# Four transformer layers: the causal mask of the last layer's second score pass moved from matmuls to a select by POOL

## The chip, the cores and the metric

The kernel runs on one core of one Trainium2 chip. The metric is the device time of the whole program in microseconds (us). An execution's time is a little longer than the span of its profile, which runs from the first to the last instruction that was recorded.

## The reference, cut to what matters

The input x is 4 sequences (B = 4) of 256 tokens with 128 features. It passes through four layers: 0 (a transformer block with full attention, 16 heads of 64), 1 (a graph attention), 2 (a conditioned attention, 16 heads of 8) and 3, the last one, where the change lies:

```python
qkv = (x @ Wqkv).reshape(b, t, 3, H, hd)          # H = 16 heads of hd = 8, t = 256
scores = jnp.einsum('bhqd,bhkd->bhqk', q, k) * scale
scores = jnp.where(causal, scores, -jnp.inf)      # causal: key <= query
attn = jax.nn.softmax(scores, axis=-1)
out = jnp.einsum('bhqk,bhkd->bhqd', attn, v)
```

followed by a projection, a residual and an MLP of 512. All of it is in float32 precision; the scores of layers 2 and 3 are products of bfloat16 parts (three parts of each operand).

## The kernel before, in words

Each attention (one layer, one sequence) has 16 heads and computes its scores twice. The **first pass** has the queries on the partitions: PE makes the scores (`scores`, L1427 to L1445) and DVE takes each query's maximum (L1132, which also gives its negative). After each group of four heads DVE turns the negated maxima into two bfloat16 parts (L1149, L1160, L1162), PE transposes them (`shift_rows`, L1461 to L1468), ACT copies them from PSUM to the tile `mT` (L957), and POOL spreads them over four heads in the rows 96 to 127 of the stacked queries (L771). The **second pass** has the keys on the partitions: one matmul per block of 128 keys gives the scores less the maxima (`scores_t`, L1470 to L1486), ACT takes the exponential into `pt` (L965), and PE multiplies `pt` with the values and a column block of ones (`values`, L1512 to L1535). DVE and ACT divide by the sums (L1168, L979, L981, L1176). Two PSUM banks are used for each pass.

In layer 3 the scores above the diagonal are masked. In the first pass a matmul of the identity with `mask_qk` (0 or -1e30) adds to the diagonal block (L1443). In the second pass the key block k meets the queries from 128 k on: key block 0 meets 256 queries, key block 1 meets 128. Each block is followed by a matmul that adds `mask_kq` to its first 128 columns, which are the diagonal block (L1485):

```python
q0 = k * 128 if layer == 3 else 0
at = k * T
dst = bk[:, at:at + T - q0]
ins = nc.tensor.matmul(dst, lhs, rhs[:, q0:T], start=True, stop=(layer == 2))
if layer == 3:
    ins = nc.tensor.matmul(bk[:, at:at + 128], identb[:], mask_kq[:], start=False, stop=True)
```

`pt` has seven slots of 128 x 512 in the layers 2 and 3, and a slot is written again only when PE has used its head (`pt_used`).

The order of the work is fixed in Python. `schedule()` makes a list of steps; in each step every running phase makes one tick. Heavy phases are the attentions, light ones are norms, projections, MLPs, the `qkv` matmuls and the graph layer. An attention has 26 steps i of two ticks each. Every engine walks the same list and so issues its instructions in this order, in order. Step i of an attention holds: first pass of head i; at i = 4, 8, 12 and 16 the transpose, the copy to `mT` and POOL's spread of the group that has just ended; second pass of head i - 6 on PE and its exponential on ACT; every fourth step the values of the four heads up to i - 8. The next attention begins while the former is at its step 15, half a step apart: in its step 4 it makes its first spread, between the former's head 13 and head 14 of the second pass. On PE the first pass of step i + 1 stands behind the second pass of step i.

POOL's queue in layer 3 is the spread (L771), preceded by a wait for everything in the dictionary `latest`, which holds POOL's own earlier results:

```python
for signal, value in latest.items():
    pool.wait_ge(signal, value)
pool.wait_ge(mT_ready, at + 1)
```

and, from light phases, `xb` (L845, once per norm) and the third part of queries and keys (L856, once per `qkv`, before DMAs by SP). POOL makes the constants at the start, `mask_kq` among them (L874, L878).

Of the kernel before, what the change touches and what calls it, by code (L numbers as in the profile page):

```python
# [17 lines left out]
NT = T // 128  # L18
# [365 lines left out]
def cond_seq_kernel(nc, x_t, adj, w0, wqk0, w1, w2, w3, wp2, wproj3, vecs, rows, out_t):  # L384
    with ExitStack() as ctx:
        def sb(name, shape, dt=F32):
            return ctx.enter_context(nc.sbuf_tensor(name, shape, dt))

        def sem(name):
            return ctx.enter_context(nc.semaphore(name))  # L390
# [15 lines left out]
        zero = sb("zero", [128, 1])  # L406
        sel = sb("sel", [128, GH, 128], BF16)
        mask_qk = sb("mask_qk", [128, 128], BF16)
        mask_kq = sb("mask_kq", [128, 128], BF16)
        mask1 = sb("mask1", [128, H, NG])  # L410
        mask2 = sb("mask2", [128, 32])
        silu = sb("silu", [128, 3, B])
# [212 lines left out]
        st_full = sem("st_full")  # L625
        pt_ready = sem("pt_ready")
        pairsum_ready = sem("pairsum_ready")
        pt_used = sem("pt_used")
        sums_ready = sem("sums_ready")
        lnsum_ready = sem("lnsum_ready")  # L630
# [61 lines left out]
        with nc.Block() as block:  # L692
# [55 lines left out]
            def _(pool):  # L748
# [3 lines left out]
                def attention(layer, b):  # L752
                    for i in range(STEPS):
                        yield
                        if 0 <= i - ST_LAG < H and layer == 0:
                            u = U_BASE[layer, b] + i - ST_LAG
                            pool.wait_ge(pt_ready, u + 1)
                            if u >= SUM_RING:
                                pool.wait_ge(pt_used, u - SUM_RING + 1)
                            nc.gpsimd.tensor_tensor(pairsum[:, u % SUM_RING, :], pt[:, pt_slot(u), 0:T],  # L760
                                                    pt[:, pt_slot(u), T:2 * T], ALU.add
                                                    ).then_inc(pairsum_ready, 1)
                            latest[pairsum_ready] = u + 1
                        g = mT_step(layer, i)
                        if g is not None and layer != 0:

                            at = G_BASE[layer, b] + g
# [3 lines that stand above are left out]
                            nc.gpsimd.tensor_copy(stacks[SHIFT_ROW:128, b % ROOMS, 0, GH * g:GH * (g + 1), :],  # L771
                                                  mT[SHIFT_ROW:128, at % 2, :].unsqueeze(1).broadcast_to(
                                                      [128 - SHIFT_ROW, GH, T])).then_inc(mT_spread, 1)
                            pool.wait_ge(mT_spread, at - FIRST_LATE_G + 1)
                        half = {ST_LAG + H // 2: 0, ST_LAG + H: 1}.get(i)
                        if layer == 0 and b >= B - ROOMS and half is not None:

                            for signal, value in latest.items():
                                pool.wait_ge(signal, value)
                            pool.wait_ge(st_full, U_BASE[layer, b] + (half + 1) * H // 2)  # L780
                            for n in range(2):
                                at = (2 * half + n) * H * T // 4
                                nc.gpsimd.memset(big[64:128, b % ROOMS, at:at + H * T // 4], 0.0
                                                 ).then_inc(stack_zero, 1)

                            zeros[0] += 2
                            pool.wait_ge(stack_zero, zeros[0])
                            if half == 1:

                                by_half = sel[SHIFT_ROW:128].unsqueeze(2).broadcast_to([128 - SHIFT_ROW, GH, NT, 128])  # L790
                                for g in range(GROUPS):
                                    keys = stacks[SHIFT_ROW:128, b % ROOMS, 1, GH * g:GH * (g + 1), :]
                                    nc.gpsimd.tensor_copy(keys.rearrange("p h (n t) -> p h n t", n=NT), by_half
                                                          ).then_inc(stack_sel, 1)
                                latest[stack_sel] = GROUPS * (b - (B - ROOMS) + 1)
                                pool.wait_ge(stack_sel, latest[stack_sel])
                        yield
# [72 lines left out]
                for at in (0, GH, DH0, DH0 + GH, SHIFT_ROW, SHIFT_ROW + GH):  # L870
                    step(nc.gpsimd.affine_select(out=sel[:], in_=sel[:], compare_op=ALU.not_equal, fill=1.0, base=-at,
                                                 pattern=[[-1, GH], [0, 128]], channel_multiplier=1))
                step(nc.gpsimd.memset(mask_qk[:], 0.0))
                step(nc.gpsimd.memset(mask_kq[:], 0.0))  # L874

                step(nc.gpsimd.affine_select(out=mask_qk[:], in_=mask_qk[:], compare_op=ALU.is_ge, fill=MASKED, base=0,
                                             pattern=[[-1, 128]], channel_multiplier=1))
                step(nc.gpsimd.affine_select(out=mask_kq[:], in_=mask_kq[:], compare_op=ALU.is_ge, fill=MASKED, base=0,  # L878
                                             pattern=[[1, 128]], channel_multiplier=-1))

                step(nc.gpsimd.memset(mask1[:], 1.0))
                step(nc.gpsimd.affine_select(out=mask1[:], in_=mask1[:], compare_op=ALU.is_ge, fill=0.0, base=0,
                                             pattern=[[-DH, H], [0, NG]], channel_multiplier=1))
# [481 lines left out]
            def _(pe):  # L1365
# [54 lines left out]
                def attention(layer, b):  # L1420
# [49 lines left out]
                    def scores_t(h):  # L1470

                        u = u_base + h
                        g, j = g_base + h // GH, h % GH
                        bk = psum[:, ST_BANK + u % 2, :]
                        pe.wait_ge(pt_ready, u - 1)
                        if j == 0:
                            pe.wait_ge(mT_spread, g - FIRST_LATE_G + 1)
                        for k in range(NT):
                            lhs, rhs = stacks[:, b % ROOMS, 1, h, k * 128:(k + 1) * 128], stacks[:, b % ROOMS, 0, h]
                            q0 = k * 128 if layer == 3 else 0  # L1480
                            at = k * T
                            dst = bk[:, at:at + T - q0]
                            ins = nc.tensor.matmul(dst, lhs, rhs[:, q0:T], start=True, stop=(layer == 2))  # L1483
                            if layer == 3:
                                ins = nc.tensor.matmul(bk[:, at:at + 128], identb[:], mask_kq[:], start=False, stop=True)  # L1485
                        ins.then_inc(st_full, 1)  # L1486

                    def turned_pair(pair):
# [23 lines left out]
                    def values(heads):  # L1512
# [9 lines left out]
                        bk = psum[:, O_BANK + o % 2, :]  # L1522
                        if heads[0] % hpo == 0 and o >= 2:
                            pe.wait_ge(o_done, o - 1)
                        pe.wait_ge(pt_ready, u_base + heads[-1] + 1)
                        for k in range(NT):
                            for h in heads:
                                at = m * (h % hpo)
                                lhs = v0[:, b % ROOMS, k, h * DH0:(h + 1) * DH0] if layer == 0 else vpad[:, vroom, k, h, :]
                                qk = k * q0  # L1530
                                ins = nc.tensor.matmul(bk[at:at + m, qk:T], lhs,  # L1531
                                                 pt[:, pt_slot(u_base + h), k * T:(k + 1) * T - qk],
                                                 start=(k == 0), stop=(k == NT - 1))
                                if k == NT - 1 and layer != 0:
                                    ins.then_inc(pt_used, 1)  # L1535
# [249 lines left out]
```

## Time and profile before

| | us |
|---|---|
| median of 3 runs | 502.93 (501.56 to 503.46) |
| the profiled execution's own time | 503.15 |
| its span | 501.4 |
| PE busy | 412.6 (82%) |
| DVE busy | 309.7 (62%) |
| ACT busy | 281.8 (56%) |
| POOL busy | 175.4 (35%) |

Busy is the time in which an engine had at least one instruction in work. Matmuls overlap each other in PE's pipeline, so that a matmul's duration is longer than the distance to the next one's start; PE's cost of a matmul is that distance. Layer 3's second pass runs from 388.8 us to 483.6 us of the span.

### The profile page before, as it was taken

To read this page: it belongs to the slowest core of one execution; us is meant where nothing else is said; L and a number is where in the kernel's file an instruction comes from. 1 tells how busy PE (TensorE), PEld (TensorE's weight loads), DVE (VectorE), ACT (ScalarE), POOL (GpSimd) and SP (SyncE) were. 2 spreads that over 40 slices of the span, in tenths; PEclk is the share of its full clock that TensorE was granted. 3 is DMA by queue.
4 is the path that set the end of the run, shared out by engine and by line. 5 is a ranking of instruction groups with operands and counts; after the bars stand their busy time and mean duration, and the time that the engine had idled before them with its cause. 6 is when DMAs were issued, how large, how long until landed. Compare 5 with 4: busy or idle time off the path is not lost. (4 is left out here: it accounts for less than half of the span.)

```text
span 501.4 us, 9353 instructions
## 1 busy us (share of the span) xinstructions
PE 412.6 (82%) x3196; PEld 262.0 (52%) x3196; DVE 309.7 (62%) x846; ACT 281.8 (56%) x597; POOL 175.4 (35%) x226
## 2 busy tenths in 40 slices
PE   2777787988989999879996979778788889798974
PEld 2534454555646556445564546344455666576643
DVE  2464686864555646655376675776888777665721
ACT  2243254446545565445755586365767666668674
POOL 2812121331155331593369330641334322321200
PEclk9999899999999999999998899797999999899998
DMA  8920033000000000120002112001322313210000
GB/s 251 248 20 1 2 37 41 8 1 1 0 1 2 0 1 1 56 61 13 0 23 66 41 57 70 3 1 31 95 68 88 99 29 100 77 64 12 3 12 10
DMA packets 34527, 21.25 MB, mean 42 GB/s; under 512 B 22832, under 2 KB 31408, under 8 KB 34096
## 3 DMA queue, kind: packets, MB, share of 16 engines
q1 hardware_dynamic: 34480, 20.65, 15.8%
q8 instruction: 26, 0.43, 0.4%
q14 instruction: 21, 0.17, 0.1%
HBM read 16.97 MB, written 3.67 MB: 41 GB/s over the span
## 5 line engine op out<-in xcount | busy, mean ns | idle before, releaser
L965 ACT ACTIVATE pt<-psum 128x512 f32<-128x512 f32 (+1 forms) x192 | 106.1, 558 | 94.0 <-PE psum L1507 46.1
L1135 DVE TENSOR_REDUCE negm<-psum 128x2 f32<-128x512 f32 x128 | 84.5, 683 | 38.3 <-PE psum L1437 23.4
L760 POOL TENSOR_TENSOR pairsum<-pt 128x256 f32<-128x256 f32 x64 | 46.7, 730 | 141.1 <-ACT pt L965 137.7
L771 POOL COPY big<-mT 32x1024 bf16<-32x1024 bf16 x32 | 33.1, 1035 | 118.7 <-ACT mT L957 118.3
L1483 PE MATMUL psum<-big 128*128 128x256 bf16 (+1 forms) x256 | 50.3, 266 | 4.6 <-POOL big L771 3.4
L1132 DVE TENSOR_REDUCE negm<-psum 128x3 f32<-128x384 f32 x64 | 34.8, 554 | 16.8 <-PE psum L1443 16.1
L1502 PE MATMUL psum<-big 64*128 64x256 f32 x256 | 39.1, 396 | 2.4 <-ACT pt L965 2.2
L1176 DVE TENSOR_TENSOR oT<-psum,rden 128x256 f32<-128x256 f32 x64 | 26.5, 414 | 17.5 <-ACT rden L981 16.9
L1406 PE MATMUL psum<-hT,pt 128*128 128x256 f32 x128 | 34.8, 409 | 2.1 <-DVE negm L1135 1.2
L1531 PE MATMUL psum<-pt,room 128*64 128x256 f32 x256 | 36.5, 408 | 0.0
L1111 DVE COPY big<-psum 128x512 f32<-128x512 f32 x32 | 22.0, 689 | 20.3 <-PE psum L1406 20.1
L1531 PE MATMUL psum<-pt,vpad 128*32 128x256 f32 (+1 forms) x512 | 32.6, 374 | 1.6 <-DVE oT L1176 1.6
L1062 DVE SCALAR_TENSOR_TENSOR xT<-psum,mods_all,xb 128x256 f32<-128x256 f32 x20 | 9.7, 483 | 35.6 <-PE psum L1602 18.7
L1483 PEld LDWEIGHTS psum<-big 128*128 128x128 bf16 x256 | 24.0, 100 | 14.4 <-ACT pt L965 5.4
L1406 PEld LDWEIGHTS psum<-hT,pt 128*128 128x128 f32 x128 | 23.6, 198 | 10.7 <-issue 4.1
L1437 PE MATMUL psum<-big 72*128 72x256 bf16 x128 | 25.9, 285 | 3.5 <-DVE negm L1135 1.9
L845 POOL TENSOR_SCALAR xb<-xT,mods_all 128x256 f32<-128x256 f32 x24 | 22.2, 928 | 17.8 <-DVE xT L1062 16.5
L1441 PE MATMUL psum<-big 72*128 72x128 bf16 (+1 forms) x128 | 25.3, 249 | 3.5 <-DVE negm L1132 3.2
L933 ACT CAST room<-big 128x512 bf16<-128x512 f32 x32 | 19.1, 612 | 14.4 <-DVE big L1111 14.4
L1502 PEld LDWEIGHTS psum<-big 64*128 64x128 f32 x256 | 19.5, 186 | 12.7 <-ACT pt L965 5.5
L981 ACT ACTIVATE rden<-rden,zero 128x256 f32<-128x256 f32 x48 | 24.4, 508 | 1.6
L1443 PE MATMUL psum<-mask_qk,identb 128*128 128x128 bf16 x128 | 25.0, 220 | 0.0
(184 smaller groups left out, 859.8 us busy)
## 6 DMA issues: line engine op xcount, KB each, us to landing
big<-scratch SPq DMA_DIRECT2D x96, 96.0 KB
scratch<-room SPq DMA_DIRECT2D x48, 64.0 KB, 2.0
adj_s<-adj SPq DMA_DIRECT2D x16, 110.0 KB, 3.9
w0s<-w SPq DMA_DIRECT2D x1, 1536.0 KB, 9.6
w3s<-w SPq DMA_DIRECT2D x1, 1088.0 KB, 12.0
room<-wqk SPq DMA_DIRECT2D x2, 512.0 KB, 6.5
xT<-x_t SPq DMA_DIRECT2D x4, 128.0 KB, 6.5
w1s<-w SPq DMA_DIRECT2D x1, 512.0 KB, 9.9
```

What stands on the lines that cost most here:

```text
L760: nc.gpsimd.tensor_tensor(pairsum[:, u % SUM_RING, :], pt[:, pt_slot(u), 0:T], pt[:, pt_slot(u), T:2 * T], ALU.add).then_inc(pairsum_ready, 1)
L771: nc.gpsimd.tensor_copy(stacks[SHIFT_ROW:128, b % ROOMS, 0, GH * g:GH * (g + 1), :], mT[SHIFT_ROW:128, at % 2, :].unsqueeze(1).broadcast_t ...
L965: nc.scalar.activation(pt[:, pt_slot(u), 0:width], psum[:, ST_BANK + u % 2, 0:width], ACT.Exp, scale=EXP_SCALE[layer]).then_inc(pt_ready, 1)
L1132: ins = nc.vector.tensor_reduce(negm[:, g, :, j], bk[:, 0:384].rearrange("p (n k) -> p n k", n=NT + 1), AX_X, ALU.max, negate=True)
L1135: ins = nc.vector.tensor_reduce(negm[:, g, 0:NT, j], bk.rearrange("p (q k) -> p q k", q=NT), AX_X, ALU.max, negate=True)
L1176: nc.vector.tensor_tensor(oT[:, b % ROOMS, c, :], psum[:, O_BANK + o % 2, 0:T], rden[:, o % 2, :], ALU.mult).then_inc(o_done, 1)
L1406: ins = nc.tensor.matmul(s_bank("G", n, b)[:, s * T:(s + 1) * T], wqk0t[:, s, 128 * n:128 * (n + 1)], hT0[:, b % H_ROOMS], start=True, sto ...
L1437: ins = nc.tensor.matmul(bk[:, q * T:(q + 1) * T], lhs, keys, start=True, stop=True)
L1441: nc.tensor.matmul(bk[:, at:at + (q + 1) * 128], lhs, keys[:, 0:(q + 1) * 128], start=True, stop=False)
L1483: ins = nc.tensor.matmul(dst, lhs, rhs[:, q0:T], start=True, stop=(layer == 2))
L1502: nc.tensor.matmul(psum[:, ST_BANK + h % 2, k * T:(k + 1) * T], qk0[half, b % ROOMS, h // 2, 1, k * 128:(k + 1) * 128], qk0[half, b % ROOM ...
L1531: ins = nc.tensor.matmul(bk[at:at + m, qk:T], lhs, pt[:, pt_slot(u_base + h), k * T:(k + 1) * T - qk], start=(k == 0), stop=(k == NT - 1))
```

## The change

In the second pass of layer 3 the two mask matmuls of each head go, and with them the tile `mask_kq` and the two instructions that make it. The two key blocks swap places in the bank and in `pt`: key block 1 (128 queries) comes first, at column 0, and key block 0 (256 queries) behind it, at column 128. The two diagonal blocks thus lie side by side in columns 0 to 255. After ACT's exponential of a head, POOL runs one `affine_select` in place on these 256 columns of `pt`, which puts 0 where the key is above the query. `values` waits for it (`pt_masked`) instead of for the exponential (`pt_ready`). The select stands in POOL's queue in step i for head i - 6, ahead of the spread of the same step, and it is entered in `latest`.

```diff
@@ gpsimd, attention @@
+                        if 0 <= i - ST_LAG < H and layer == 3:
+
+                            u = U_BASE[layer, b] + i - ST_LAG
+                            pool.wait_ge(pt_ready, u + 1)
+                            diagonals = pt[:, pt_slot(u), 0:T].rearrange("p (n q) -> p n q", n=NT)
+                            nc.gpsimd.affine_select(out=diagonals, in_=diagonals, compare_op=ALU.is_ge, fill=0.0, base=0,
+                                                    pattern=[[0, NT], [1, 128]], channel_multiplier=-1
+                                                    ).then_inc(pt_masked, 1)
+                            latest[pt_masked] = u - U_BASE[3, 0] + 1
@@ gpsimd, constants @@
-                step(nc.gpsimd.memset(mask_kq[:], 0.0))
-                step(nc.gpsimd.affine_select(out=mask_kq[:], in_=mask_kq[:], compare_op=ALU.is_ge, fill=MASKED, base=0,
-                                             pattern=[[1, 128]], channel_multiplier=-1))
@@ tensor, scores_t @@
-                            at = k * T
-                            dst = bk[:, at:at + T - q0]
-                            ins = nc.tensor.matmul(dst, lhs, rhs[:, q0:T], start=True, stop=(layer == 2))
-                            if layer == 3:
-                                ins = nc.tensor.matmul(bk[:, at:at + 128], identb[:], mask_kq[:], start=False, stop=True)
+                            at = k * T if layer == 2 else 128 - q0
+                            ins = nc.tensor.matmul(bk[:, at:at + T - q0], lhs, rhs[:, q0:T], start=True, stop=True)
@@ tensor, values @@
-                        pe.wait_ge(pt_ready, u_base + heads[-1] + 1)
+                        if layer == 3:
+                            pe.wait_ge(pt_masked, u_base - U_BASE[3, 0] + heads[-1] + 1)
+                        else:
+                            pe.wait_ge(pt_ready, u_base + heads[-1] + 1)
...
+                                p0 = 128 - qk if layer == 3 else k * T
                                 ins = nc.tensor.matmul(bk[at:at + m, qk:T], lhs,
-                                                 pt[:, pt_slot(u_base + h), k * T:(k + 1) * T - qk],
+                                                 pt[:, pt_slot(u_base + h), p0:p0 + T - qk],
                                                  start=(k == 0), stop=(k == NT - 1))
```

## Rows read from the trace of the kernel before

**Rows 1.** Busy time by stretch: PE, PEld, DVE, ACT, POOL, then clock, DMA.

```profile
420.00:440.00 20.00, 16.51 (x154) 12.04 (x152) 12.44 (x39) 14.33 (x34) 5.16 (x5) 0.91 0.32 92
460.00:480.00 20.00, 18.65 (x203) 13.62 (x203) 13.54 (x44) 14.87 (x32) 4.04 (x4) 1.00 0.01 2
```

**Rows 2.** Waits from 385 to 486: waiter, releaser, us, times, longest.

```profile
ACT pt L965 <- PE psum L1485: 10.1, 16, 1.2
PE psum L1483 <- POOL big L771: 2.9, 5, 1.2
```

**Rows 3.** Timeline: the first and the last of eight spreads, each with the next matmul.

```profile
398.47 1.03 POOL L771 COPY big<-mT 32x1024 bf16<-32x1024 bf16 x1 [1.96 <-ACT mT L957]
...
399.65 0.27 PE L1483 MATMUL psum<-big 128*128 128x256 bf16 x1
...
480.30 1.04 POOL L771 COPY big<-mT 32x1024 bf16<-32x1024 bf16 x1 [6.76 <-ACT mT L957]
...
481.49 0.27 PE L1483 MATMUL psum<-big 128*128 128x256 bf16 x1 [1.19 <-POOL big L771]
```

**Rows 4.** Timeline of one cycle of four heads: start, us, instruction.

```profile
457.83 1.04 POOL L771 COPY big<-mT 32x1024 bf16<-32x1024 bf16 x1 [7.01 <-ACT mT L957]
...
459.01 0.27 PE L1483 MATMUL psum<-big 128*128 128x256 bf16 x1 [0.61 <-POOL big L771]
...
459.12 0.22 PE L1485 MATMUL psum<-mask_kq,identb 128*128 128x128 bf16 x1
459.17 0.22 PE L1483 MATMUL psum<-big 128*128 128x128 bf16 x1
...
459.40 1.01 DVE L1132 TENSOR_REDUCE negm<-psum 128x3 f32<-128x384 f32 x2
459.51 0.22 PE L1443 MATMUL psum<-mask_qk,identb 128*128 128x128 bf16 x1
...
460.86 0.17 DVE L1162 TENSOR_TENSOR m<-negm,m 128x8 bf16<-128x8 f32 x1
...
461.17 0.27 PE L1466 MATMUL psum<-identb,m 128*128 128x128 bf16 x2
...
461.48 0.36 ACT L957 COPY mT<-psum 32x256 bf16<-32x256 bf16 x1 [0.94 <-PE psum L1466]
...
461.87 0.49 ACT L965 ACTIVATE pt<-psum 128x384 f32<-128x384 f32 x1
...
462.00 1.04 POOL L771 COPY big<-mT 32x1024 bf16<-32x1024 bf16 x1 [3.13 <-ACT mT L957]
```

**Rows 5.** Timeline: a spread (one of four) that PE reaches late.

```profile
443.30 1.04 POOL L771 COPY big<-mT 32x1024 bf16<-32x1024 bf16 x1 [9.13 <-ACT mT L957]
...
446.04 0.27 PE L1483 MATMUL psum<-big 128*128 128x256 bf16 x1
```

**Rows 6.** Timeline of POOL at the start, each waiting for the one before.

```profile
15.99 0.29 POOL L876 TENSOR_SCALAR_AFFINE_SELECT mask_qk<-mask_qk 128x128 bf16<-128x128 bf16 x1
16.43 0.29 POOL L878 TENSOR_SCALAR_AFFINE_SELECT mask_kq<-mask_kq 128x128 bf16<-128x128 bf16 x1
```

**Rows 7.** POOL's selects in the groups by line and shape.

```profile
L871 POOL TENSOR_SCALAR_AFFINE_SELECT sel<-sel 128x512 bf16<-128x512 bf16 x6 | 3.8, 634 | 0.9
L876 POOL TENSOR_SCALAR_AFFINE_SELECT mask_qk<-mask_qk 128x128 bf16<-128x128 bf16 x1 | 0.3, 292 | 0.1
```

**Rows 8.** Timeline behind the spread at 449.78, where the MLP follows.

```profile
450.96 0.27 PE L1483 MATMUL psum<-big 128*128 128x256 bf16 x1
...
451.96 1.97 PE L1616 MATMUL psum<-hL,w3s 128*128 128x256 f32 x8 [0.28 <-ACT hL L921]
```

**Rows 9.** Timeline of the last values.

```profile
484.84 0.47 ACT L965 ACTIVATE pt<-psum 128x384 f32<-128x384 f32 x1
484.96 0.42 DVE L1176 TENSOR_TENSOR oT<-psum,rden 128x256 f32<-128x256 f32 x1 [1.19 <-ACT rden L981]
...
485.45 0.86 PE L1531 MATMUL psum<-pt,vpad 128*32 128x256 f32 x16 [1.62 <-DVE oT L1176]
```

**Rows 10.** Timeline: a POOL instruction and a DVE instruction at once.

```profile
385.48 1.16 POOL L856 TENSOR_TENSOR room<-room 128x512 bf16<-128x512 f32 x1 [2.87 <-ACT room L1049]
385.50 1.17 DVE L1162 TENSOR_TENSOR m<-negm,m 128x8 bf16<-128x8 f32 x1
```

More of the change, by code:

```diff
@@ L408, in cond_seq_kernel @@
         mask_qk = sb("mask_qk", [128, 128], BF16)
-        mask_kq = sb("mask_kq", [128, 128], BF16)
         mask1 = sb("mask1", [128, H, NG])
@@ L627, in cond_seq_kernel @@
         pairsum_ready = sem("pairsum_ready")
+        pt_masked = sem("pt_masked")
         pt_used = sem("pt_used")
```

## The prediction, made before the changed kernel ran

> **What bounds the kernel now.** I read the busy times by stretch first. In the last layer PE is busy for 18.65 of 20 us, ACT 14.87, DVE 13.54 and POOL only 4.04 [rows 1]. That looks like a stage bound by PE with an idle POOL, and on such a reading taking matmuls from PE and giving POOL a select is a gain. But PE's busy time counts the latency of each matmul, so I went to the waits and the timeline of the layer. PE waits for POOL's spread L771 in five places, 2.9 us in all [rows 2], and only waits above a threshold are listed. In the timeline I took all 16 spreads of layer 3 and put beside each the first second-pass matmul of its group. In eight of them the matmul starts 1.18 to 1.19 us after the spread does, which is the spread's 1.03 us and a reaction: PE goes as soon as POOL is done. The first is at 398.47, the last at 480.30 [rows 3], another at 457.83 [rows 4]. (A ninth and a tenth, at 387.64 and 462.00, are as tight, but are the first of their attention; below.) In four others PE comes much later: the spread of 443.30 ends at 444.34 and the matmul starts at 446.04 [rows 5].
>
> So layer 3 is a ring, not one engine. Its plain form is the cycle from 457.83 to 462.00, 4.17 us for four heads: spread by POOL, second pass of the group's first head on PE (459.01), behind it in PE's queue the first pass of the next head (ends 459.51 + 0.22), its maximum on DVE (the pair ends 460.41), the three small DVE steps (to 461.03), the transpose 461.17, the copy to mT 461.48, and the next spread 462.00 [rows 4].
>
> **What the change removes.** 128 mask matmuls, two per head. A mask matmul of 459.12 is followed by the next matmul at 459.17 [rows 4], so it costs PE's stream about 0.055 us, 0.11 per head, 64 x 0.11 = 7.0 us in all. How much of it is on the path? ACT waits for L1485, the last matmul of the second pass, 10.1 us in 16 places [rows 2], but that head's end comes only 0.11 earlier each time, at most 16 x 0.11 = 1.8 us. In the step that matters most, where the spread is made, ACT does the copy to mT first (461.48 to 461.84) and goes straight on with the exponential at 461.87 [rows 4]: it isn't PE that holds it, nothing is gained. In the eight cycles that aren't lengthened (next part) the ends of the range are 0 and 8 x 4 x 0.11 = 3.5 us. I take 1.4 us: where projections and norms stand between the heads, PE runs from one matmul to the next and about 0.2 to 0.3 us of the 0.44 is on the path; in the plain cycle none. The constants at the start lose a memset and a select (0.29 us and the wait to the next, 15.99 to 16.43 [rows 6]); POOL is ahead there and I count 0. Swapping the key blocks changes no count and no length: 0.
>
> **What it adds.** 64 selects of 256 float32 columns. The trace has none of this shape: a select of 128 columns took 292 ns, one of 512 took 634 [rows 7]. These are the ends; in between by length, 292 + 128 x 0.89 = 406 ns. I take 0.41 us. In sum 26 us more for an engine that has 16 us free in 20 [rows 1]: load isn't the matter, place is.
>
> By the Trainium skill, page "GPSIMD Engine Reference", section "Performance versus the Vector engine", a body with few operations takes 1.03 cycles per element; at the 1.2 GHz that the skill gives this is an estimate of 0.22 us. The rows' slope of 0.89 ns per element is near that rate, the rest is a fixed part that the rows show and the figure leaves out. With 0.22 in place of 0.41 the sum below would be some 1.5 us less.
>
> In POOL's queue the select of head i - 6 stands ahead of the spread of step i, and waits for that head's exponential. The exponential ends at 462.36; the copy to mT, for which alone the spread waits now, ends at 461.84 [rows 4]. The spread is then late by 0.52 + 0.41 + the wait for the select's own end, which is 0.15 at most (16.28 to 16.43 [rows 6]); I take 0.1. Together 1.03, say 1.0 us (bounds 0.9 to 1.3). This holds for the spreads at steps 8, 12 and 16, twelve in layer 3. At step 4 the select ahead is that of the former attention's head 13, whose exponential is long done, or there is none: four spreads aren't late. Of the twelve, four have the room seen in [rows 5] (1.7 us there), and eight are the tight ones.
>
> What the 1.0 us becomes in each of the eight depends on what follows. In the plain cycle behind 457.83 the first pass of the next head is late by 1.0 less the 0.11 of two masks, ends at 460.62, and its maximum, which was half a microsecond behind because DVE had two of them in a row, ends at about 461.25 in place of 460.41: 0.84 us, all of it handed to the next spread. Where the MLP or the qkv matmuls follow, PE waits for ACT now and 0.28 of it is idle [rows 8]: L1616 starts at 451.96, 1.00 after the head; with the head 1.0 late and 0.11 shorter it starts at about 452.5, then another two masks go before the next transpose: 0.45 us. There are four of this kind (399 to 480), 0.35 to 0.45 each, 1.65 in all. Two have norm work of DVE in between (after 398.47 and 428.36), where I read 0.1 and 0.25. Behind the last one, 480.30, no work is left to hide it.
>
> There the change adds its second wait. The last exponential ends at 485.31, DVE's product at 485.38, and the values start at 485.45 [rows 9]. With the select the values start at 485.31 + 0.41 + two reactions of 0.07 (as 485.38 to 485.45), 485.86, plus what ACT is late. From the spread 1.0 us late, less masks and PE's wait for ACT, 0.5 arrives at that exponential: in all 1.0 us for the end. Elsewhere the values come two steps after the exponential and the select is done: 0.
>
> Sum of delays: 0.84 + 1.65 + 0.35 + 1.0 = 3.8 us.
>
> **DVE beside POOL.** While POOL ran the two-input L856 from 385.48 for 1.16 us, DVE's L1162, 8 columns wide and 0.17 us elsewhere [rows 4], took 1.17 and ended with it [rows 10]. A select that meets L1160 or L1162, which lie on the ring, could hold DVE up to 0.41 us. Bounds: 0, and 16 x 0.41 = 6.6 us. Selects fill about a third of POOL's time and half of the cycles hang on DVE, so I take 0.8.
>
> The Trainium skill, page "GPSIMD Engine Reference", section "Key points", says that GPSIMD shares its SBUF interfaces with VectorE, with contention for VectorE instructions of two SBUF inputs or in a 2-port mode. By that rule, the trace agrees for L1162; whether a one-input select does the same to it no row shows, and it is the second rival.
>
> **Sum.** 3.8 + 0.8 - 1.4 = +3.2 us. The profiled execution took 503.15 us with a span of 501.4; it becomes 506.35. The median of the three runs is 0.2 below that execution, so I predict 506.1 us.
>
> **Rivals.**
> 1. PE's stream is the bound between the spreads, as its 18.65 of 20 [rows 1] suggests. Then all 64 x 0.11 = 7.0 us come back while the delays stay 3.8: -3.2, 499.7 us, faster. It decides for this one if more than 0.07 us of each head's 0.11 is on the path (4.6 of 7.0). Against it: plain cycles show PE idle before L1466 and L1483 [rows 4].
> 2. The shared read: POOL's selects hold DVE in nearly every group, 6.6 in place of 0.8: +9.0, 511.9 us.
> 3. The waits absorb more than I read, above all in the cycles with light work, so that only the plain cycle and the end are late: 0.84 + 1.0 - 1.4 = +0.4, 503.3 us, no change. For it: only five waits for POOL are long enough to be listed [rows 2].
>
> A fall of the granted clock is a side effect that I can't size: 420 to 440 already has 0.91 [rows 1], and a PE with 4 us more of waits could fall once more, for about 1 us.
>
> **How the numbers follow.** Forecast 0.55, rival 1 0.13, rival 2 0.12, rival 3 0.20. Half a per cent, 2.5 us, is what a measurement here can tell from no change: below 500.4 is faster, above 505.4 slower. Within the forecast (504 to 508.5) about seven in ten lie above 505.4: 0.40 + 0.12 gives slower 0.52; same 0.15 + 0.20 = 0.35; faster 0.13. The range is 500.5 to 510.0: most of the forecast and of rival 3, half of the way to rivals 1 and 2.
>
> **What would show it.** Right: 64 selects of about 0.41 us; the twelve spreads of steps 8 to 16 starting 1.0 us or more after the copy to mT ends, in place of 0.16; PE's waits for L771 grown from 2.9 to some 8 us; the plain cycle 5.0 us long in place of 4.17; the last values 0.55 or more after the last exponential. Wrong: spreads that start at once (another order in the queue), first spreads of an attention late too, cycles with the MLP shorter than before, L1160 or L1162 of 0.4 us and more in most groups (rival 2), or a layer 3 that runs from 388 to 486 in the same time although the spreads are late (rival 3).

## The result: 0.6% slower, and the profile after

The changed kernel took 504.94 us (median of 22 runs, 502.62 to 509.73) against 502.51 us of 22 runs of the kernel before. The ratio is 1.0059, with a 95% interval of 1.004 to 1.0078: 2 to 4 us slower. (All ratios here leave out executions over 1.5% above the fastest of their kernel.) The prediction was 506.1 us, slower with 0.52. It was right in direction and nearly in size, but **its main step was wrong, and the front of this document has the same mistake**: it says that the select stands in POOL's queue ahead of the spread of the same step. It stands behind it. The diff's first hunk begins after `pool.wait_ge(mT_spread, ...)`, the line that ends the spread's block, and `if 0 <= i - ST_LAG < H and layer == 3:` follows that. What this means for each term is told below; an experiment ran the order that I had assumed.

| | before | after |
|---|---|---|
| profiled execution | 503.15 | 504.12 |
| span | 501.4 | 502.3 |
| PE busy | 412.6 | 406.5 |
| DVE, ACT busy | 309.7, 281.8 | 310.4, 281.0 |
| POOL busy | 175.4 | 200.4 |

POOL's select in the groups by line and shape of the changed kernel (count, busy, mean ns, idle before). It is the 0.41 us that was worked out from the ends of [rows 7]:

```profile
L780 POOL TENSOR_SCALAR_AFFINE_SELECT pt<-pt 128x256 f32<-128x256 f32 x64 | 25.9, 407 | 35.9 <-ACT pt L970 33.5
```

The waits from 385 to 486 of the changed kernel, which answer to [rows 2]. L771 is the spread, L780 the select, L1487 the second pass, L1537 the values:

```profile
POOL pt L780 <- ACT pt L970: 33.5, 28, 4.3
POOL big L771 <- ACT mT L962: 11.6, 14, 2.1
ACT pt L970 <- PE psum L1487: 9.3, 13, 1.6
...
PE psum L1537 <- POOL pt L780: 4.6, 6, 2.2
...
PE psum L1487 <- POOL big L771: 3.6, 5, 1.5
```

PE's waits for the spread have hardly grown (2.9 to 3.6 us; 8 was forecast), and without any select (e1 below) they are 4.2 us, so the growth is no work of the select. A new one stands above them: the values wait for the select, 4.6 us in six places. These are all: 16 groups of four heads have their values in layer 3, and in the other ten the select had ended at least 1.3 us before. (The texts written ahead of the runs e2, e5, e8 and e0 count seven; the traces have six.)

The plain cycle of four heads in the changed kernel, the same one as in [rows 4], by its timeline (start, us, instruction):

```profile
457.84 1.03 POOL L771 COPY big<-mT 32x1024 bf16<-32x1024 bf16 x1 [0.37 <-ACT mT L962]
...
458.94 1.87 POOL L780 TENSOR_SCALAR_AFFINE_SELECT pt<-pt 128x256 f32<-128x256 f32 x4
...
459.02 0.33 PE L1487 MATMUL psum<-big 128*128 128x256 bf16 x2 [0.82 <-POOL big L771]
...
459.41 1.01 DVE L1137 TENSOR_REDUCE negm<-psum 128x3 f32<-128x384 f32 x2
...
460.03 0.86 PE L1537 MATMUL psum<-pt,vpad 128*32 128x256 f32 x16 [0.22 <-POOL pt L780]
460.46 0.36 DVE L1154 TENSOR_TENSOR negm<-negm 128x4 f32<-128x4 f32 x1
...
461.38 0.27 PE L1471 MATMUL psum<-identb,m 128*128 128x128 bf16 x2
...
461.69 0.36 ACT L962 COPY mT<-psum 32x256 bf16<-32x256 bf16 x1 [1.35 <-PE psum L1471]
...
462.07 0.49 ACT L970 ACTIVATE pt<-psum 128x384 f32<-128x384 f32 x1
...
462.21 1.03 POOL L771 COPY big<-mT 32x1024 bf16<-32x1024 bf16 x1 [1.40 <-ACT mT L962]
```

The spread still starts 0.16 us after the copy to mT (461.69 + 0.36 to 462.21), as before, and ahead of the exponential's end at 462.56. The reader is to see two small losses. The values at 460.03 wait for the select although the two mask matmuls of each of two heads are gone: 0.09 later than before after all. And DVE's L1154, which takes 0.165 us when left alone, takes 0.36: it ends at 460.82, and POOL's row of four selects ends at 460.81. The cycle is 4.37 us long in place of 4.17.

The longest wait inside the layer. Timeline of the changed kernel, POOL and the values:

```profile
430.34 1.03 POOL L771 COPY big<-mT 32x1024 bf16<-32x1024 bf16 x1 [2.11 <-ACT mT L962]
431.45 0.41 POOL L780 TENSOR_SCALAR_AFFINE_SELECT pt<-pt 128x256 f32<-128x256 f32 x1
431.82 1.15 POOL L865 TENSOR_TENSOR room<-room 128x512 bf16<-128x512 f32 x1
432.93 0.41 POOL L780 TENSOR_SCALAR_AFFINE_SELECT pt<-pt 128x256 f32<-128x256 f32 x1
433.48 0.86 PE L1537 MATMUL psum<-pt,vpad 128*32 128x256 f32 x16 [1.16 <-POOL pt L780]
```

The exponential of the group's last head had ended at 431.92. The select that the values need stands behind the spread, another select and L865 (the third part of queries and keys), which a light phase puts into POOL's queue.

And the end, which answers to [rows 9]:

```profile
484.80 0.47 ACT L970 ACTIVATE pt<-psum 128x384 f32<-128x384 f32 x1
484.92 0.42 DVE L1181 TENSOR_TENSOR oT<-psum,rden 128x256 f32<-128x256 f32 x1 [1.11 <-ACT rden L986]
485.33 0.41 POOL L780 TENSOR_SCALAR_AFFINE_SELECT pt<-pt 128x256 f32<-128x256 f32 x1 [0.82 <-ACT pt L970]
485.88 0.86 PE L1537 MATMUL psum<-pt,vpad 128*32 128x256 f32 x16 [2.20 <-POOL pt L780]
486.67 3.38 PE L1608 MATMUL psum<-oT,wproj3s 128*128 128x256 f32 x8
```

**Why one profile against one profile isn't enough here.** Beside the rows above, the two traces differ by where the granted clock was at its lower level of 1.2 GHz in place of 2.4, and that moves from execution to execution. Busy time by stretch, layer 3 up to its last exponential and from there to the end (PE, PEld, DVE, ACT, POOL, then the granted clock): first before, then after, then a second kernel that differs from before only by the place of the blocks (e9 below):

```profile
387.60:485.30 97.70, 84.84 (x900) 61.71 (x900) 64.93 (x206) 70.08 (x156) 24.40 (x24) 0.98 0.17 52
485.30:501.40 16.10, 9.06 (x44) 6.24 (x44) 3.37 (x12) 6.23 (x12) 0.92 (x1) 0.89 0.02 8
```

```profile
388.80:485.30 96.50, 78.20 (x772) 52.96 (x772) 65.69 (x206) 69.58 (x156) 49.52 (x87) 0.98 0.18 52
485.30:502.30 17.00, 10.08 (x44) 6.84 (x44) 3.32 (x12) 6.23 (x11) 1.33 (x2) 0.80 0.02 8
```

```profile
390.90:487.00 96.10, 83.26 (x900) 60.51 (x900) 64.80 (x206) 69.79 (x156) 24.35 (x24) 1.00 0.17 52
```

With the clock at 1.00 throughout, the 15 distances between the 16 spreads repeat in e9 to 0.01 us those of before, but for one: 8.64 us from the ninth spread to the tenth where before has 10.17 (from 433.13 to 443.30, [rows 5]), with the clock low inside. So the stage without such a stretch is 96.1 us before. The two profiles of the changed kernel (96.5 and, in e0 below, 96.2) each have one low stretch, at different spreads (6.50 for 5.31 there, 14.31 for 13.37 here); taking it out by the other profile's distances gives 95.3 us for both. **By these traces the stage up to the last exponential is 0.8 us shorter with the change, and the end 1.0 longer (17.0 for 16.0 or 16.1)**, of which 0.5 is the select (the last values start 0.6 us after the last exponential, before 0.14) and the rest that the clock was low around L1608 in both profiles of the change. Two kernels without a select (e1 and e10) have a low clock in the end too, for which they take 16.7 and 17.0 us, so this rest isn't shown to be the change's. The stage's start moves between 385.6 and 392.4 over the 14 profiles, although the work before it differs by a few constants at most: it is at 387.6 in before and at 390.9 in e9, which has the same work up to there.

### The profile page after: what moved, and what is told of

It is laid out like the page before. It is cut to its first block and busy times, and to the rows that moved or that the text cites. A ratio compares the mean times of both kernels' runs of the same rounds, so it can differ in the third digit from the quotient of the medians.

```text
span 502.3 us, 9166 instructions
## 1 busy us (share of the span) xinstructions
PE 406.5 (81%) x3068; PEld 253.8 (51%) x3068; DVE 310.4 (62%) x846; ACT 281.0 (56%) x597; POOL 200.4 (40%) x288
## 5 line engine op out<-in xcount | busy, mean ns | idle before, releaser
L771 POOL COPY big<-mT 32x1024 bf16<-32x1024 bf16 x32 | 33.1, 1034 | 72.3 <-ACT mT L962 71.4
L1487 PE MATMUL psum<-big 128*128 128x256 bf16 (+1 forms) x256 | 47.8, 271 | 5.2 <-POOL big L771 4.1
L780 POOL TENSOR_SCALAR_AFFINE_SELECT pt<-pt 128x256 f32<-128x256 f32 x64 | 25.9, 407 | 35.9 <-ACT pt L970 33.5
L1537 PE MATMUL psum<-pt,vpad 128*32 128x256 f32 (+1 forms) x512 | 33.3, 380 | 4.6 <-POOL pt L780 4.6
L1537 PE MATMUL psum<-pt,room 128*64 128x256 f32 x256 | 36.5, 408 | 0.0
L1487 PEld LDWEIGHTS psum<-big 128*128 128x128 bf16 x256 | 22.1, 101 | 16.2 <-ACT pt L970 7.0
L1446 PE MATMUL psum<-big 72*128 72x128 bf16 (+1 forms) x128 | 25.5, 251 | 4.6 <-DVE negm L1137 4.2
L1411 PEld LDWEIGHTS psum<-hT,pt 128*128 128x128 f32 x128 | 23.6, 198 | 10.7 <-issue 4.1
```

The costliest lines, as they stand in the source:

```text
L780: nc.gpsimd.affine_select(out=diagonals, in_=diagonals, compare_op=ALU.is_ge, fill=0.0, base=0, pattern=[[0, NT], [1, 128]], channel_multi ...
L1411: ins = nc.tensor.matmul(s_bank("G", n, b)[:, s * T:(s + 1) * T], wqk0t[:, s, 128 * n:128 * (n + 1)], hT0[:, b % H_ROOMS], start=True, sto ...
L1487: ins = nc.tensor.matmul(bk[:, at:at + T - q0], lhs, rhs[:, q0:T], start=True, stop=True)
L1537: ins = nc.tensor.matmul(bk[at:at + m, qk:T], lhs, pt[:, pt_slot(u_base + h), p0:p0 + T - qk], start=(k == 0), stop=(k == NT - 1))
```

## The experiments

The ratios are to executions of the kernel before that were taken beside them; 2.5 us are 0.5%.

The traces give a second and finer measure. Twelve of the 15 distances between spreads (all but the third, eighth and ninth) are free of low clock in every profile but those of e3 and e8. Their sum repeats to 0.01 us where a kernel was profiled twice, or differs by the swap alone. In us, with the time from the last exponential to the last values:

| | 12 distances | to the last values |
|---|---|---|
| before; e9 (swap alone) | 72.40; 72.39 | 0.14; 0.14 |
| the change; e0 (the same again) | 71.64; 71.63 | 0.62; 0.62 |
| e1, no mask and no select | 70.98 | 0.14 |
| e4, select that nobody waits for | 71.03 | 0.14 |
| e7, last head of each group by matmul | 71.40 | 0.14 |
| e2, both masks | 73.32 | 0.62 |
| e10, values later, no select | 69.99 | 0.14 |
| e5, values later, with the select | 68.93 | 0.62 |

**e9, the swap alone.**

```diff
-                            at = k * T
+                            at = k * T if layer == 2 else 128 - q0
...
+                                p0 = 128 - qk if layer == 3 else k * T
```

> The kernel before with the key blocks swapped in the bank and in pt, and nothing else: mask matmuls, no select. My prediction: 0. Theory: within 0.5 us of before. Rival L (the place of the blocks matters, for instance because the last matmul of the second pass now writes another part of the bank): up to 1 us either way.

Ratio 0.9999 (0.996 to 1.0038). The swap costs nothing, as forecast.

**e1, no mask at all in the second pass.** It leaves the mask of this pass out, and the exponential's scale is smaller.

```diff
-EXP_SCALE = {0: float(DH0) ** -0.5, 2: 1.0, 3: float(DH) ** -0.5}
+EXP_SCALE = {0: float(DH0) ** -0.5, 2: 1.0, 3: 1.0e-3}
...
-                            nc.gpsimd.affine_select(out=diagonals, ...).then_inc(pt_masked, 1)
...
-                            pe.wait_ge(pt_masked, ...)
...
+                        pe.wait_ge(pt_ready, u_base + heads[-1] + 1)
```

> The change without its select: the second pass of layer 3 has no mask at all (neither matmuls nor select), the values wait for the exponential as before; the exponential's scale in layer 3 is 0.001 so that nothing overflows. It is the gain of the removal alone. Theory W (the change costs by what the values wait for the select, and saves little): 1.0 to 2.5 us faster than before, about 501. Rival P (PE's stream bounds the layer, each head's 0.11 us counts): 4 to 7 us faster, 496 to 498. Rival N (the masks' matmuls lie wholly in the shade of other waits): within 0.5 us of before.

Ratio 0.9965 (0.9929 to 1.0001): 1.8 us faster, 0 to 3.6. In its profile 14 of the 15 distances between spreads (all but the one with a low clock) sum to 1.4 us less than in e9. The plain cycle stays at 4.17. So a fifth to a quarter of the 7.0 us of matmuls was on the path: theory W. Rival P (4 to 7 us) falls; rival N lies inside the ratio's interval, and it is the distances that speak against it.

**e2, both masks.** The change with the mask matmuls and their constant back in.

```diff
...
+                            if layer == 3:
+                                ins = nc.tensor.matmul(bk[:, at:at + 128], identb[:], mask_kq[:], start=False, stop=True)
```

> The change with the mask matmuls left in: PE's work is that of before, the select and the values' wait for it come on top. Theory W: 3 to 5 us slower than before (values wait for a select in seven of 16 groups, 3.2 us more than before in the profile, and DVE is held for 0.9 us), about 506.5. Rival P: the same as the change plus what the matmuls cost, 4 to 7 us more than the change, about 510. Rival N: the same as the change, 505.

Ratio 1.0118 (1.007 to 1.0166): 5.9 us slower than before, some 3 above the change and a little above theory W's 3 to 5. The stage took 97.3 us at a clock of 1.00 throughout, 1.2 above e9 and 2.0 above the change: the select with its waits costs that 1.2 us of the stage, and the matmuls' removal beside it gives 2.0 back. Rival N falls. P's 510 us are a ratio of 1.014, inside the interval; against P stand e1 and the 2.0 us of the stage. The other 4.7 us of the measured 5.9 are not in this stage; its profile is longer before it (the stage starts at 392.4) and after it (18.7 us, clock low).

**e3, the select ahead of the spread**, the order of the prediction.

```diff
-(behind the spread's block)
+                        if 0 <= i - ST_LAG < H and layer == 3:
+                            ... affine_select ...
                         g = mT_step(layer, i)
                         if g is not None and layer != 0:
```

> The select stands ahead of the spread of the same step in POOL's queue, the order that my prediction assumed by mistake. By the prediction's sum: eight tight spreads 1.0 us late each, of which 2.8 us remain before the end and 1.0 at the end: in all +3.2 us on before, 506. Theory W: spreads at steps 8, 12 and 16 start 1.0 us after the copy to mT in place of 0.16, and it is slower than the change by 1 to 3 us: 506 to 508. Rival Q (the order in POOL's queue doesn't matter): as the change, 505.

Ratio 1.0214 (1.0162 to 1.0266): 10.7 us slower than before, more than any theory said. Its timeline in the cycle behind the same spread as above:

```profile
461.15 0.36 ACT L962 COPY mT<-psum 32x256 bf16<-32x256 bf16 x1
...
461.54 0.49 ACT L970 ACTIVATE pt<-psum 128x384 f32<-128x384 f32 x1
...
462.10 0.41 POOL L769 TENSOR_SCALAR_AFFINE_SELECT pt<-pt 128x256 f32<-128x256 f32 x1 [0.60 <-ACT pt L970]
...
462.75 1.04 POOL L780 COPY big<-mT 32x1024 bf16<-32x1024 bf16 x1 [0.24 <-POOL pt L769]
...
463.93 0.33 PE L1487 MATMUL psum<-big 128*128 128x256 bf16 x2 [1.90 <-POOL big L780]
```

The spread starts 1.24 us after the copy to mT has ended, in exactly twelve of 16 places; the first ones of the four attentions start after 0.16. The mechanism is as the prediction described it for this order, 1.08 us in place of 1.0. Its price was not. The waits are

```profile
PE psum L1487 <- POOL big L780: 11.3, 9, 2.4
...
PE psum L1537 <- POOL pt L769: 1.1, 3, 0.6
```

and the granted clock fell with them:

```profile
387.70:492.00 104.30, 83.10 (x772) 56.66 (x772) 66.14 (x206) 70.21 (x156) 49.76 (x87) 0.90 0.16 48
492.00:510.20 18.20, 11.22 (x44) 7.68 (x44) 3.35 (x12) 6.23 (x11) 1.33 (x2) 0.71 0.03 8
```

Nine of its 15 distances between spreads are free of low clock; they are 3.9 us longer in all than the change's, and 2.2 of this is twice the step from a spread in time to a late one, which the next spread in time gives back. The six with low clock are 5.1 us longer, although all the steps back are in them. So most of the loss lies where the clock was low; how much of it is the clock's own stays open.

**e4, the select elsewhere.** POOL selects on a tile of its own, no mask is applied, PE waits for the exponential alone.

```diff
...
-                            diagonals = pt[:, pt_slot(u), 0:T].rearrange("p (n q) -> p n q", n=NT)
+                            diagonals = other[:, n % 3, :].rearrange("p (n q) -> p n q", n=NT)
```

> POOL runs the 64 selects at the same places and after the same exponentials, but on a tile of its own; no mask is applied in the second pass, and the values wait for the exponential alone. Scale as in the run without a mask, with which it is to be compared. Theory W (the wait is what costs): 0.5 to 1.2 us slower than that run (DVE held by selects, spreads behind selects), still faster than before or equal. Rival S (shared read and POOL's queue cost, not the wait): 3 us slower than the run without a mask, as slow as the change.

Ratio 1.0024 (0.9985 to 1.0063), 3 us above e1, but the intervals of the two overlap. DVE is held in the same eight places as in the change (six times L1154, twice the cast behind it), without anybody waiting for the select: the hold is POOL's running, not the data. The ratio doesn't separate the wait from the rest: by it two thirds or more of the select's cost is there without the wait, by its interval anything from none to all. The trace does, for layer 3 at the upper clock: the twelve distances are 71.03 us against 70.98 in e1, so 64 selects with their holds of DVE cost next to nothing there in sum (each plain cycle is 4.38 in place of 4.17, and light cycles are shorter), and with the values' wait (the change) they are 71.64.

**e7, every fourth head by matmul.**

```diff
...
+                            by_pe = layer == 3 and h % 4 == 3
...
+                            if by_pe:
+                                ins = nc.tensor.matmul(bk[:, at:at + 128], identb[:], mask_kq[:], start=False, stop=True)
```

> The change, but in each group of four heads the last one (3, 7, 11, 15) is masked by matmuls as before and has no select. The values of a group then wait for the select of a head whose exponential lies a step earlier, and for the last head's exponential. Theory W (the values' wait for the last select is the cost): the waits of the values for POOL go, 2 to 4 us faster than the change, 501 to 502.5, equal to before or a little faster. Rival S (shared read, queue and the rest): a quarter of the selects gone, at most 1 us faster than the change.

Ratio 0.998 (0.9947 to 1.0013), 0.8%, some 3.9 us, below the change's 1.0059; the two intervals don't overlap (they do with e0's, 0.9998 to 1.0071). No wait of the values for POOL is listed any more, three quarters of the selects are still there, and 1.8 us of matmuls are back on PE. DVE is held as in the change: seven times L1154's instruction and once the cast, 1.2 us over their usual length (1.1 in the change). This is the clearest run for theory W: the late select of a group's last head is what cost. Its trace has less than the ratio: 0.2 us in the twelve distances and 0.5 at the end. The rest is in the granted clock, as told under what stays open.

**e8, every select twice.**

```diff
...
+                            pool.wait_ge(pt_masked, 2 * (u - U_BASE[3, 0]) + 1)
+                            nc.gpsimd.affine_select(out=diagonals, in_=diagonals, ...).then_inc(pt_masked, 1)
```

> The change, with every select done twice, one after the other (the second changes nothing); the values wait for the second. 0.41 us and a gap of 0.07 more per head before the values may start, POOL busy for 30 us more. Theory W: the seven waiting groups wait about 0.5 more each, 3.4 us, and the four groups whose last select begins just behind another select 0.5 more again, DVE is held more often: 4 to 7 us slower than the change, 509 to 512. Rival S: the holds of DVE double, 1 to 2 us slower than the change.

Ratio 1.0245 (1.0196 to 1.0294), 12.3 us above before and 9 above the change, beyond theory W's 4 to 7. Waits from 385 to 490 and the stage's clock in its profile:

```profile
PE psum L1541 <- POOL pt L784: 6.9, 5, 2.1
PE psum L1491 <- POOL big L771: 5.4, 9, 1.7
```

```profile
387.90:493.40 105.50, 81.79 (x772) 55.35 (x772) 68.13 (x206) 69.86 (x156) 74.22 (x150) 0.93 0.17 48
493.40:513.60 20.20, 12.71 (x44) 8.67 (x44) 3.36 (x12) 6.24 (x12) 1.74 (x3) 0.67 0.02 6
```

**e5, the values later**: the select gets time in place of being made shorter.

```diff
...
                             scores(i)
+                        if layer == 3 and 0 <= i - 1 - PV_LAG < H and (i - 1 - PV_LAG) % 4 == 3:
+                            values(range(i - PV_LAG - 4, i - PV_LAG))
...
-                        if 0 <= i - PV_LAG < H and (i - PV_LAG) % n == n - 1:
+                        if layer != 3 and 0 <= i - PV_LAG < H and (i - PV_LAG) % n == n - 1:
```

> The change, with the values of layer 3 issued on PE after the first pass of the next head, a good third of a us later in PE's queue, so that the select has that much more time. Theory W: three of the seven waits are 0.29 us and go, the others get shorter by 0.3, but the values and the sums come later: 0.5 to 1.5 us faster than the change, 503.5 to 504.5. Rival S: as the change, 505, or slower by the sums' delay.

Ratio 0.9932 (0.9895 to 0.9968): 3.4 us faster than before where at best 503.5 us, a little slower, was expected. The plain cycle in its timeline, with the first pass (L1446) now ahead of the values and the select done 0.5 us before them:

```profile
456.42 1.87 POOL L780 TENSOR_SCALAR_AFFINE_SELECT pt<-pt 128x256 f32<-128x256 f32 x4
...
457.50 0.23 PE L1446 MATMUL psum<-big 72*128 72x128 bf16 x1 [0.21 <-DVE negm L1137]
...
457.89 0.86 PE L1537 MATMUL psum<-pt,vpad 128*32 128x256 f32 x16
```

It is as long as in the change, 4.37 us: DVE's L1154 is held just the same. The gain lies in the cycles with light work.

**e10, the values later without the select.** The same move in the kernel before (mask matmuls).

> The kernel before (mask matmuls, no select), with the values of layer 3 issued behind the first pass of the next head, as in the run e5_values_later. It tells whether that run's 0.7% below before comes from hiding the select or from the order of PE's queue alone. Theory O (order): the four first passes of a group end earlier on PE, DVE's maxima and the next spread with them; 3 to 5 us faster than before, 498 to 500, so that the select on top costs some 2 us. Rival H (hiding): within 1 us of before, and the order is worth something only with the select.

Ratio 0.9944 (0.9907 to 0.9982), 2.8 us, just below theory O's 3 to 5. The ratio alone is weak: the medians of all executions, 502.19 and 502.47, are only 0.3 us apart. The trace is clear: at an upper clock throughout, its stage from the first spread to the last exponential takes 93.7 us where e9 has 96.1; one of its distances between spreads, for instance, is 4.92 us where before has 5.69. So most of e5's gain is the order of PE's queue, theory O. With the values moved, select or matmuls make no difference that the ratios can tell (0.9932 and 0.9944). The twelve distances do tell one: 68.93 us with the select, 69.99 with the matmuls. Once the select is hidden, the change does shorten these distances, by 1.1 us, and still loses 0.5 at the end.

**e11 and e12**, e5 with the last head of every group by matmul, and e5 with only the very last group so.

> Both: the values behind the next first pass, and the last head of each group of four masked by matmuls, so that the values wait for no late select. Theory W: the last waits of e5_values_later (2.8 us in three places, of which 0.4 is the end's and about 0.9 the other two's) go: 1 us faster than e5_values_later, about 500. Rival S: as e5_values_later.

> The values behind the next first pass, and only the very last group of four heads (sequence 3) masked by matmuls. Theory: the end's wait of 0.4 us goes and nothing else changes: 0.3 to 0.6 us faster than e5_values_later, which such a comparison can't tell from it; in the profile the last values start 0.15 after DVE's product instead of 0.57.

Ratios 0.9923 (0.9888 to 0.9958) and 0.9928 (0.9895 to 0.9961), both below e5 by less than can be told. In e12 the last values start 0.07 us after DVE's product (478.61 to 478.68), as before the change. The intervals of both lie below 1 and below the change's.

**e0, the change again.**

> The change itself once more, on the same chip and beside the same runs of before as the three others: 1.004 to 1.008 times before, about 505.5; and a second profile of it, in which the values wait for the select in the same seven groups, whatever the clock does.

Ratio 1.0034 (0.9998 to 1.0071): lower than the first 1.0059, with which it overlaps, and just under the 1.004 expected. The values waited in the same six groups, with the same 4.6 us.

## Why the prediction was right or wrong, point by point

- **The eight late spreads (0.84 + 1.65 + 0.35, and the lateness that reached the end): the step that failed.** No spread waits for the select of its own step, since the select stands behind it. 15 of 16 start within 0.28 us of the end of the copy to mT; one starts 0.78 after it, behind two selects and an `xb`, and the room behind it takes that up (the next distance is 7.7 us in place of 8.6). A reading of one line of the diff, not of the trace, made this term. The prediction had named the sign itself: "spreads that start at once (another order in the queue)".
- **What stood in its place** was declared 0 in the prediction ("the values come two steps after the exponential and the select is done"). In six of 16 groups the select was not done: PE stood idle for it for 0.2 to 1.2 us in five groups inside the layer, and the last values start 0.5 later than they would. The runs: e7 takes that wait away, with DVE held as before, and gains 0.8%; e4 keeps the selects, drops the wait, and has the twelve distances of a kernel without selects; e2 shows what wait and holds cost with PE's work unchanged. In plain words, that the sum came near was luck: one term wasn't there and another was missed.
- **The size of the failed term was wrong too.** For the order assumed the sum was +3.2 us; e3 measured +10.7. The lateness per spread was right (1.08). The fall of the clock, named with about 1 us but left out of the sum, was real: 0.90 in the stage. How much of the miss is the clock and how much is lateness that wasn't absorbed stays open (the distances under e3).
- **The removal: right.** 1.4 us were taken for the cycles that aren't lengthened and 0.11 to 0.22 in each of the others, some 2 in all; e1 measured 1.8 (0 to 3.6), and e2 against the change 2.0 in the stage.
- **The select's length: right**, 407 ns for 406. The estimate from the rate in the Trainium skill, page "GPSIMD Engine Reference", section "Performance versus the Vector engine", was 0.22; the measured 407 ns decides: the rate alone is too little for so short an instruction.
- **DVE beside POOL: the hold was right, its price isn't borne out.** 0.8 us were taken; eight instructions of the ring were held for 1.1 us in all (0.2 before). But e4 has the same holds, and its twelve distances are those of e1, which has no select. The rule of the Trainium skill that was weighed (page "GPSIMD Engine Reference", section "Key points"), contention for VectorE's instructions with two SBUF inputs, agrees with the trace for a one-input select too: L1154, a tensor_tensor, ends with it.
- **The end: 1.0 forecast, 1.0 in the profile**, but by 0.5 of select and a low clock, not by lateness brought along. That too is luck.
- **Rival 1** (PE's stream decides) falls by e1. **Rival 2** (holds in every group) falls by the profile. **Rival 3** (the waits absorb it) is nearer than its 0.20 said: in the traces alone, layer 3 and the end together cost the change 0.2 us.

**Where the measured 2 to 4 us are, and what stays open.** At an upper clock the traces give the change no loss: 0.8 us gained in the twelve distances, 0.5 lost at the end. The mean granted clock of every execution is on record, and the rest is there. It is below 0.96 in 29 of the change's 34 executions (with e0) and in 20 of the 86 of the kernel before that were taken beside the experiments; the means are 0.953 and 0.964. At equal clock the two take the same time: between 0.95 and 0.96 it is 504.6 us for the change and 504.7 before (17 and 13 executions), between 0.96 and 0.97 it is 502.9 and 502.6 (5 and 54). So the slowdown is that more of the program runs at the lower clock.

What lowers it is less sure. With the matmuls gone and no select (e1) the clock is 0.963, so it isn't the missing matmuls. With the select and its wait it is lower also when the matmuls stay (e2, 0.956). With the late selects gone (e7) it is 0.965 again. These point to PE's waits for the select. e4, selects without the wait, lies between (0.958) and decides nothing, and e9, where nothing waits, has 0.959: means of twelve executions are sure to some 0.003 each, e2's of six to 0.004. Why waits of about 1 us and less should do it no run shows.

## What to carry to other kernels

Place each added instruction in its engine's queue by the lines around the hunk, and then ask who waits for it in each place of the queue: POOL was idle for two thirds of the time, and what cost was the last select of a group, which ended 0.5 us and more after the exponential that the consumer used to wait for. Before an operation in a producer's chain is shortened, try whether the consumer can stand one piece of independent work later in its queue: here the move alone made the layer 2.4 us shorter (e10, at equal clock), and it turned the change from 1.0059 to 0.9932 (e5). And where two profiles have their low clock in different places, compare them cycle by cycle over stretches of equal clock, not span by span, and compare the granted clock of all executions beside their times.

## What the runs showed of the hardware that was not expected

- A one-input select on POOL held a two-input DVE instruction on SBUF that began while it ran until it ended: 0.28 to 0.36 us for 0.165, in six of 15 places, whichever tile the select works on (e4). One that had begun 0.05 us before the select took its 0.165. A cast to bfloat16 (one input) was held too, 0.28 to 0.30 us for 0.17; the one-input BATCH_NORM_AGGREGATE (0.17 us) wasn't, and ended 0.1 us before the select in whose time it began.
- PE's waits seem to cost twice. Where those for the spread grew to 11.3 us (e3), the granted clock of layer 3 was 0.90 in place of 0.98 to 1.00, and 0.71 in place of 0.89 at the end; the stage with twelve spreads late by 1.08 us each became 8.2 us longer than e9's. Over all executions e3's and e8's mean clocks are the lowest, 0.947 and 0.944, for 0.964 before. That the waits are the cause is argued from this order, not shown by itself.
- With the clock at its upper level a cycle repeats to 0.01 us from execution to execution (twelve of them sum to 72.40 and 72.39 us, or to 71.64 and 71.63); what varies by microseconds is where the clock is low: the same cycle of 8.64 us took 10.17 with a low stretch in it.
